# Mix weights of the first two blocks from one on-chip table, quantizer units in their order of use, block 1's gate and up products beside block 0's

## The chip, the core and the metric

The kernel runs on one core of one Trainium2 chip. TensorE multiplies, VectorE (DVE) and ScalarE (ACT) do the work on rows, GpSimd (POOL) has small jobs, SyncE (SP) and ScalarE issue the transfers. The metric is the time of one execution in microseconds on the device. Lower is better.

## The reference, cut to what matters

```python
x: (64 samples, 64 channels, 512)           # 4096 rows of 512
# layer 0
y  = einsum('bct,bcd->bdt', x, weights[subjects])      # each sample has one of 8 64x64 matrices
w  = ternary_quant(w_gate_up), ternary_quant(w_proj)   # groups of 64: mean of |w|, sign, scale
h  = silu(gate) * up                                   # hidden size 2048
x  = x + rms_norm(h) @ wq_p.T
# layer 1
H  = x @ W.T + adapter (rank 16, one of 8 per sample)
x  = x + sum over 8 experts of c[t, e, o] * (H @ expert_w[e].T + expert_b[e])
     # c: softmax of a 4096-column router, top 2 of 8, renormalized
```

## The kernel before, in words

The rows are worked in 8 blocks of 512 (`NBLK`). Stage A, some 850 us, computes layer 0 for a block and, behind it, the layer-1 linear of the block before. The router and the experts follow and are not touched. All float products are made of high and low halves ("hi" and "lo"), which ScalarE (hi) and VectorE (lo) split off.

A block is: `mix` (the sample matrices, two uses of a PSUM slot), then for each of the 16 hidden chunks j `gu(i, j)` (16 matmuls, gate and up), `silu` of the gate on ScalarE, the product on VectorE, the split of the product (`high`, `low`), its square and the running sum (`square`, `squares`), and `proj(i, j)` (8 matmuls) into four PSUM banks. At the end come `squares(i)` (TensorE's sums over columns), the variance, `power` on GpSimd, the residual, `turn` (transposes), `adapt` and two `linear` halves for layer 1.

**Blocks 0 and 1 are special.** The weights arrive unquantized. `UNITS` lists 24 units of 1,024 columns: "up" j (the gate and up weights of chunk j) and "down" (projection weights of two chunks). A unit is loaded, ScalarE makes magnitude and sign (`quant_in`), TensorE the group mean (`quant`, 2 matmuls), VectorE the scale (`quant_scale`, or `quant_floor` where ScalarE has copied the mean out in `quant_mean`), two gap instructions (`quant_gap`) and three more (`quant_sign`), and ScalarE writes the result out (`quant_out`). The loop over `h` in `range(PAIRS)` (8 passes) does this for three units a pass, with the `gu` and `proj` of block 0 for two chunks. Block 1's `gu` rides along one pass late: pass h has `gu(0, 2h)`, `gu(1, 2h - 2)`, `gu(0, 2h + 1)`, `gu(1, 2h - 1)`; the last two (`AHEAD = 2`) come after the loop. Block 1's products are kept as tiles `hid1` in a ring of 6; ten of them go to memory (`keep_hid`) and are fetched again (`fetch_hid`). After the loop TensorE projects block 1 in the order `SECOND_ORDER` (chunks 10 to 14, then 0 to 9, then 15): `proj(1, p)`. Positions 5 to 14 take fetched tiles.

**What sets the order.** Every engine's program is written out by hand; an engine works strictly in that order. `slot` is a ring of two PSUM slots; `FIRST`, `SECOND`, `REST` number its uses. A use n waits until `drained` counts n - 1, that is, until the use two before it is read out (`take`). For instance the `gu` of chunk 1 uses the slot of the fourth group mean.

**Mix weights.** `mixw` (block 0) and `mixw1` (block 1) are block-diagonal, one 64x64 matrix for each sample. `gather_mix` on SyncE reads a sample's index into a register (`value_load`) and issues one 16 KB transfer from memory (L452, L454); four of block 0's eight come from GpSimd in the same way (L691, L693).

**Transfers.** SyncE has the units' loads, the gathers, `keep_hid` and, at the end of the loop, this sequence (L500 to L509), which the change leaves alone:

```python
for r in range(5):
    fetch_hid(r)
sp.wait_ge(w_lo_ready, 3)          # wc_lo of linear_weights is written
sp.dma_start(x_mix[:, :, :], one(XB, 2)).then_inc(xmix_in, 16)
gather_mix(2, mixw, mixw_in)
for r in range(5, HC - RING):
    fetch_hid(r)                   # tile of position 5 + r
```

`linear_weights` splits the layer-1 weights, which lie in `x_mix`, into `wc_hi` and `wc_lo`; `small_weights` does the adapter's.

## Time and profile before

| | us |
|---|---|
| median of 3 runs | 2211.55 (2211.19 to 2212.24) |
| the profiled execution | 2213.71 |
| its span | 2212.0 |
| TensorE busy | 2193.9 (99%) |
| VectorE busy | 1625.1 (73%) |
| ScalarE busy | 1053.5 (48%) |
| GpSimd busy | 63.8 (3%) |

TensorE is busy nearly throughout, so the time is its instructions plus what it loses at the start and in a few waits. Two stretches differ from the rest: the first 40 us, in which the first weights have to arrive, and the quantizing loop (to about 177 us), in which VectorE is nearly full too. "Granted clock" is the share of 2.4 GHz that TensorE got: 1.00 or 0.50.

### The profile page before, as it was taken

Reading aid. Unit: us, or ns where it says so; the run is one execution under the profiler, and the core shown is the slowest. Engines: PE = TensorE matmul, PEld = TensorE weight load, DVE = VectorE, ACT = ScalarE, POOL = GpSimd, SP = SyncE. Lnnn points to the kernel's source line nnn. Section 1 sums busy time; section 2 is a strip of 40 time slices with the busy share of each in tenths; the row PEclk is TensorE's granted clock in tenths of the full one; section 3 lists DMA queues with packets and bytes.
Section 4 is the critical chain, followed back from the end, with each engine's and each line's share of the span. In section 5 each row is a group of like instructions: output and inputs, shape, how many; then the busy total and the mean of one; then the engine's idle time right before and its main releaser. Section 6 shows DMA issues by size and latency. Waiting matters only on the chain.

```text
span 2212.0 us, 28768 instructions
## 1 busy us (share of the span) xinstructions
PE 2193.9 (99%) x9817; PEld 1810.9 (82%) x9817; DVE 1625.1 (73%) x2119; ACT 1053.5 (48%) x1493; POOL 63.8 (3%) x83
## 2 busy tenths in 40 slices
PE   7999999999999999999999999999999999999999
PEld 5778888888888888888888888888888888888887
DVE  8986444444444445689999999999898888888883
ACT  6764333333333233588777878777332222222221
POOL 0000000101111102000000000000000000000000
PEclk9999999999999999999999999999999999999999
DMA  6313303232424224412212121116222222222220
GB/s 210 105 53 126 98 20 105 83 107 81 111 80 109 92 58 143 157 67 81 81 71 85 71 85 71 63 68 262 103 100 85 81 85 81 95 71 100 66 85 24
DMA packets 157908, 205.66 MB, mean 93 GB/s; under 512 B 63330, under 2 KB 96674, under 8 KB 155682
## 3 DMA queue, kind: packets, MB, share of 16 engines
q1 hardware_dynamic: 114578, 149.95, 20.5%
q10 hardware_dynamic: 43152, 55.06, 7.6%
q8 instruction: 22, 0.36, 0.1%
q14 instruction: 28, 0.23, 0.0%
q0 software_dynamic: 128, 0.07, 0.0%
HBM read 136.35 MB, written 68.68 MB: 93 GB/s over the span
## 4 chain that ended last, share of the span: by engine, by line
PE 94%; issue 4%; DVE 1%; POOL 1%; ACT 0%; DMA 0%; POOLq 0%; DVEq 0%; ACTq 0%
PE slot L1657 19%; PE ex_bank L1834 10%; PE ex_bank L1833 10%; PE ex_bank L1832 10%; PE pj L1670 9%; PE high_bank L1799 5%; PE high_bank L1803 5%; PE high_bank L1801 5%; PE low_bank L1799 4%; PE low_bank L1803 4%; PE low_bank L1801 4%; PE slot L1719 3%; PE slot L1626 1%; PE slot L1708 1%; PE ex_bank L1847 1%
## 5 line engine op out<-in xcount | busy, mean ns | idle before, releaser
L1657 PE MATMUL slot<-y_hi,wgu 128*128 128x512 f32 x1024 | 402.5, 393 | 1.2 <-ACT wgu L768 0.6
L1657 PE MATMUL slot<-y_lo,wgu 128*128 128x512 f32 x1024 | 399.3, 390 | 0.0
L1832 PE MATMUL ex_bank<-ew_hi,hb 128*128 128x512 f32 x992 | 385.9, 389 | 0.0
L1833 PE MATMUL ex_bank<-ew_hi,hb 128*128 128x512 f32 x992 | 385.9, 389 | 0.0
L1834 PE MATMUL ex_bank<-ew_lo,hb 128*128 128x512 f32 x992 | 385.9, 389 | 0.0
L1104 ACT ACTIVATE ex_bank<-eb_sb 128x512 f32<-128x512 f32 x248 | 149.3, 602 | 451.1 <-DVE acc L1563 391.5
L1513 DVE SCALAR_TENSOR_TENSOR lead_in<-code_in,wts 128x1024 bf16<-128x1024 bf16 x256 | 311.7, 1218 | 7.5 <-ACT wts L1044 5.8
L1657 PEld LDWEIGHTS slot<-y_hi,wgu 128*128 128x128 f32 x1024 | 192.8, 188 | 44.8 <-DVE q_scale L1174 2.9
L1657 PEld LDWEIGHTS slot<-y_lo,wgu 128*128 128x128 f32 x1024 | 192.7, 188 | 39.8
L1216 DVE TENSOR_TENSOR hid<-gate,slot 128x512 f32<-128x512 f32 x112 | 76.9, 687 | 192.0 <-ACT gate L784 191.3
L1832 PEld LDWEIGHTS ex_bank<-ew_hi,hb 128*128 128x128 f32 x992 | 186.2, 188 | 38.7
L1833 PEld LDWEIGHTS ex_bank<-ew_hi,hb 128*128 128x128 f32 x992 | 186.2, 188 | 38.6
L1834 PEld LDWEIGHTS ex_bank<-ew_lo,hb 128*128 128x128 f32 x992 | 186.2, 188 | 38.6
L784 ACT ACTIVATE gate<-slot 128x512 f32<-128x512 f32 x128 | 76.3, 596 | 276.5 <-PE slot L1657 237.3
L1799 PE MATMUL high_bank<-rw_hi,hb 128*128 128x512 f32 x512 | 199.3, 389 | 0.0
L1803 PE MATMUL high_bank<-rw_lo,hb 128*128 128x512 f32 x512 | 199.2, 389 | 0.0
L1801 PE MATMUL high_bank<-rw_hi,hb 128*128 128x512 f32 x512 | 199.2, 389 | 0.0
L1563 DVE SCALAR_TENSOR_TENSOR acc<-ex_bank,c_ring,acc 128x512 f32<-128x512 f32 x193 | 144.6, 749 | 66.0 <-PE ex_bank L1834 63.2
L1670 PE MATMUL pj<-wpj,hid_hi 128*128 128x512 f32 x484 | 190.1, 393 | 0.0
L1670 PE MATMUL pj<-wpj,hid_lo 128*128 128x512 f32 x484 | 188.4, 389 | 0.0
L1799 PE MATMUL low_bank<-rw_hi,hb 128*128 128x512 f32 x384 | 149.4, 389 | 0.0
L1801 PE MATMUL low_bank<-rw_hi,hb 128*128 128x512 f32 x384 | 149.4, 389 | 0.0
(169 smaller groups left out, 3500.8 us busy)
## 6 DMA issues: line engine op xcount, KB each, us to landing
hb<-h_scratch SPq DMA_DIRECT2D x34, 512.0 KB, 3.3
code_scratch<-half_code SPq DMA_DIRECT2D x32, 512.0 KB, 2.6
half_in<-code_scratch SPq DMA_DIRECT2D x32, 512.0 KB, 3.3
hb<-h_scratch ACTq DMA_DIRECT2D x30, 512.0 KB, 3.6
h_scratch<-ht ACTq DMA_DIRECT2D x48, 256.0 KB, 3.0
q_raw<-in_w_ffn SPq DMA_DIRECT2D x21, 512.0 KB, 3.4
x_scratch<-x_res ACTq DMA_DIRECT2D x8, 1024.0 KB, 4.5
lead_scratch<-lead SPq DMA_DIRECT2D x32, 256.0 KB, 2.0
```

The lines of the kernel that those rows point to most:

```text
L1104: nc.scalar.activation(ex[e][:, :], eb_sb[:, e, :], ACT.Copy).then_inc(ex_seeded, 1)
L1216: nc.vector.tensor_tensor(hid[:, j % 2, :], gate[:, g, :], slot[s % 2][:, 1, :], ALU.mult).then_inc(drained, 1)
L1513: nc.vector.scalar_tensor_tensor(lead_in[:, k % 2, :].bitcast(BF16).rearrange("p (a n) -> p a n", a=2), code_in[:, k % 2, :, :], float(2 * ...
L1563: nc.vector.scalar_tensor_tensor((res if e == E - 1 and not first else acc)[:, u, :], ex[e][:, :], c_ring[:, k, e:e + 1], (xin if e == 0 e ...
L1657: last = mm(slot[s % 2][:, g, :], wgu[:, c, r * P:(r + 1) * P], y[:, c, :], start=(c == 0 and v == 0), stop=(c == DC - 1 and v == 1))
L1670: last = mm(pj[k][:, :], h[:, k * P:(k + 1) * P], wpj[:, w, :], start=(j == 0 and v == 0), stop=(j == HC - 1 and v == 1))
L1799: mm(plane[k][:, :], hb[:, u, c, 0, :], rw_hi[:, k, c, :], start=False, stop=False, skip_group_check=True)
L1801: mm(plane[k][:, :], hb[:, u, c, 1, :], rw_hi[:, k, c, :], start=False, stop=False, skip_group_check=True)
L1803: last = mm(plane[k][:, :], hb[:, u, c, 0, :], rw_lo[:, k, c, :], start=False, stop=True, skip_group_check=True)
L1832: mm(ex[e][:, :], hb[:, u, c, 0, :], ew_hi[:, e, c, :], start=False, stop=False, skip_group_check=True)
L1833: mm(ex[e][:, :], hb[:, u, c, 1, :], ew_hi[:, e, c, :], start=False, stop=False, skip_group_check=True)
L1834: last = mm(ex[e][:, :], hb[:, u, c, 0, :], ew_lo[:, e, c, :], start=False, stop=(c == DC - 1), skip_group_check=True)
```

## The change

- **Table.** The whole table of 8 matrices is loaded once into each half of the partitions (two transfers of 128 KB, pieces of 256 bytes). For blocks 0 and 1 the matrices are then copied on chip with a register as index: four samples on VectorE, twelve on GpSimd. The twelve transfers of SyncE and the four of GpSimd go. Blocks 2 to 7 gather as before.
- **Loads.** SyncE issues block 1's rows (`x_res`) as soon as unit 0 has landed, and unit 2 behind them; ScalarE's queue keeps units 0 and 1 and `x_mix`.
- **Units** stand in the order up 2h, up 2h + 1, down h.
- **Order.** Both mixes come before unit 1's group mean. `gu(1, j)` follows `gu(0, j)` at once, in every pass, and `AHEAD` is gone. ScalarE copies two group means a pass. In the first pass VectorE puts block 1's low halves between gap and sign of unit 1, and all of unit 2 behind the first two products.
- **PSUM.** The first blocks use `slot_first` and `pj_first` (block 1's mix is written into the latter, with the semaphores `mix1_filled` and `mix1_drained`); later uses have them in exchanged places. `bank` chooses. The router's and experts' banks are renamed to match.
- **Second block.** Without `gu` behind the loop, `proj(1, 0)` follows the sums of squares. The residual of block 0 is put between the low halves; `small_weights` goes into the loop, `linear_weights` from before position 4 to behind position 6; `turn`, `adapt` and `linear` on TensorE move from positions 1, 2, 5, 7, 10 to 3, 4, 8, 10, 13.

```diff
-UNITS = [u for j in range(HC) for u in ([("up", j), ("down", j // 2)] if j % 2 == 0 else [("up", j)])]
+UNITS = [u for h in range(HC // 2) for u in (("up", 2 * h), ("up", 2 * h + 1), ("down", h))]
...
-FIRST = ["q0", "q1", "mix0@0", "mix1@0", "q2"]
+FIRST = ["q0", "mix0@0", "mix1@0", "q1"]
...
+    FIRST += [f"gu{_j}@0", f"gu{_j}@1"]
+    FIRST += ["q2"] if _h == 0 else []
     FIRST += [f"q{k}" for k in quant_of(_h)[:2]]
...
+    FIRST += [f"gu{_j + 1}@0", f"gu{_j + 1}@1"]
     FIRST += [f"q{k}" for k in quant_of(_h)[2:]]
```

SyncE's program:

```diff
-            sp.wait_ge(dconst, 2)
-            sp.wait_ge(subject_in, 16)
-            gather_mix(0, mixw, mixw_in, range(SPB // 2))
+            for r in range(0, P, C):
+                sp.dma_start(table[r:r + C, :, :], cond_w.rearrange("(v r) k -> r v k", r=C)).then_inc(table_done, 16)
...
+            sp.wait_ge(qraw_in[0], 16)
             sp.dma_start(x_res[:, :, :], one(XB, 1)).then_inc(xmix1_in, 16)
-            gather_mix(1, mixw1, mixw1_in, range(3))
+            sp.dma_start(q_raw[:, 2, :], w_ffn[2]).then_inc(qraw_in[2], 16)
```

GpSimd's (VectorE has the same for its four samples, before unit 0):

```diff
+            pool.wait_ge(table_done, 32)
+
+            def choose(i, w, samples, done):
+                for q in samples:
+                    v = pool.value_load(subject_i[0:1, i * SPB + q:i * SPB + q + 1], min_val=0, max_val=E - 1)
+                    r = (q % 2) * C
+                    nc.gpsimd.tensor_copy(w[r:r + C, q // 2, r:r + C],
+                                          table[r:r + C, bass.ds(v, 1), :].rearrange("p z k -> p (z k)")).then_inc(done, 1)
+
+            choose(0, mixw, range(SPB // 2, SPB), first_chosen)
+            choose(1, mixw1, range(SPB), second_chosen)
```

TensorE's:

```diff
             quant(0)
             again(9)
+            mix(0)
+            second_mix()
             quant(1)
-            mix(0)
-            quant(2)
...
                 gu(0, j)
-                if h:
-                    gu(1, j - 2)
+                gu(1, j)
+                if h == 0:
+                    quant(2)
...
                 gu(0, j + 1)
-                if h:
-                    gu(1, j - 1)
-                else:
-                    mix(1)
+                gu(1, j + 1)
                 proj(0, j)
...
-            for j in range(HC - AHEAD, HC):
-                gu(1, j)
             for p in range(HC - 1):
                 proj(1, p, SECOND_ORDER[p])
-                if p in (1, 2):
-                    turn(0, p - 1)
-                if p == 5:
+                if p in (3, 4):
+                    turn(0, p - 3)
+                if p == 8:
                     adapt(0)
-                if p == 7:
+                if p == 10:
                     linear(0, 0)
-                if p == 10:
+                if p == 13:
                     linear(0, 1)
```

The order of ScalarE and VectorE is shown as their instructions stand. In the names, `y_hi` and `y_lo` are halves of a mix, `gate` is a silu, `q_mag` and `q_sign` a `quant_in`, `wgu` and `wpj` a `quant_out`.

ScalarE at the start, before, from unit 0's write-out to block 0's first gate and the two write-outs behind it:

```order
L768 ACTIVATE wgu<-q_res 128x4x256
L747 ACTIVATE y_hi<-slot 128x1024 x2
L754 ACTIVATE q_mag<-q_raw 128x1024
L755 ACTIVATE q_sign<-q_raw 128x1024
L754 ACTIVATE q_mag<-q_raw 128x1024
L755 ACTIVATE q_sign<-q_raw 128x1024
L754 ACTIVATE q_mag<-q_raw 128x1024
L755 ACTIVATE q_sign<-q_raw 128x1024
L784 ACTIVATE gate<-slot 128x512
L771 ACTIVATE wpj<-q_res 128x1024
L768 ACTIVATE wgu<-q_res 128x4x256
```

The same place in the change:

```order
L755 ACTIVATE y_hi<-slot_first 128x1024 x2
L783 ACTIVATE wgu<-q_res 128x4x256
L762 ACTIVATE y_hi<-pj_first 128x1024 x2
L769 ACTIVATE q_mag<-q_raw 128x1024
L770 ACTIVATE q_sign<-q_raw 128x1024
L783 ACTIVATE wgu<-q_res 128x4x256
L769 ACTIVATE q_mag<-q_raw 128x1024
L770 ACTIVATE q_sign<-q_raw 128x1024
L769 ACTIVATE q_mag<-q_raw 128x1024
L770 ACTIVATE q_sign<-q_raw 128x1024
L799 ACTIVATE gate<-slot_first 128x512
L818 ACTIVATE sq<-hid 128x512
```

The first gate had no write-out before it but unit 0's; now unit 1's `wgu` and the `quant_in` of units 3 and 4 behind it stand ahead of it.

VectorE at the start, before, from block 0's low halves of the mix to the second scale behind the first product:

```order
L1167 TENSOR_TENSOR y_lo<-slot,y_hi 128x1024 x2
L1174 TENSOR_SCALAR q_scale<-slot 128x1024
L1187 TENSOR_TENSOR q_gap<-q_scale,q_mag 128x1024
L1191 TENSOR_TENSOR q_res<-q_gap,q_mag 128x1024
L1197 TENSOR_TENSOR q_gap<-q_gap,q_mag 128x1024
L1199 TENSOR_TENSOR q_res<-q_res,q_gap 128x1024
L1202 TENSOR_TENSOR q_res<-q_res,q_sign 128x1024
L1216 TENSOR_TENSOR hid<-gate,slot 128x512
L1174 TENSOR_SCALAR q_scale<-slot 128x1024
```

The same place in the change:

```order
L1200 TENSOR_TENSOR y_lo<-slot_first,y_hi 128x1024 x2
L1214 TENSOR_SCALAR q_scale<-slot_first 128x1024
L1227 TENSOR_TENSOR q_gap<-q_scale,q_mag 128x1024
L1231 TENSOR_TENSOR q_res<-q_gap,q_mag 128x1024
L1207 TENSOR_TENSOR y_lo<-pj_first,y_hi 128x1024 x2
L1237 TENSOR_TENSOR q_gap<-q_gap,q_mag 128x1024
L1239 TENSOR_TENSOR q_res<-q_res,q_gap 128x1024
L1242 TENSOR_TENSOR q_res<-q_res,q_sign 128x1024
L1256 TENSOR_TENSOR hid<-gate,slot_first 128x512
L1264 TENSOR_TENSOR hid<-gate,slot_first 128x512
L1214 TENSOR_SCALAR q_scale<-slot_first 128x1024
L1227 TENSOR_TENSOR q_gap<-q_scale,q_mag 128x1024
```

Unit 1 is now done around block 1's low halves, and unit 2 (here its first two instructions) moved behind both first products.

VectorE in the second block, before, from the sum of position 3 to the low half of position 4 (`hid1` is block 1's tile; L1160 is `wc_lo`):

```order
L1249 TENSOR_TENSOR sumsq<-sumsq,sq 128x512
L1224 TENSOR_TENSOR hid1<-gate,slot0 128x512
L1143 TENSOR_TENSOR a_lo<-a_raw,a_hi 128x512
L1145 TENSOR_TENSOR b_lo<-b_raw,b_hi 128x512
L1149 TENSOR_SCALAR adapter_i<-adapter_i 128x1
L1150 CAST lmask<-idx_i 128x64
L1152 CAST adapter_f<-adapter_i 128x1
L1154 TENSOR_SCALAR lmask<-lmask,adapter_f,scal_sb 128x64
L1160 TENSOR_TENSOR wc_lo<-x_mix,wc_hi 128x2048
L1238 TENSOR_TENSOR hid_lo<-hid1,hid_hi 128x512
```

And in the change, from the low half of position 4 (L1194 is `wc_lo`):

```order
L1278 TENSOR_TENSOR y_lo<-hid1,y_hi 128x512
L1289 TENSOR_TENSOR sumsq<-sumsq,sq 128x512
L1278 TENSOR_TENSOR y_lo<-hid1,y_hi 128x512
L1289 TENSOR_TENSOR sumsq<-sumsq,sq 128x512 x3
L1278 TENSOR_TENSOR hid_lo<-hid1,hid_hi 128x512
L1289 TENSOR_TENSOR sumsq<-sumsq,sq 128x512
L1194 TENSOR_TENSOR wc_lo<-x_mix,wc_hi 128x2048
L1278 TENSOR_TENSOR hid_lo<-hid1,hid_hi 128x512
```

The split of the layer-1 weights stood before position 4's low half and now stands behind position 6's sum.

## Rows read from the trace of the kernel before

**Rows 1.** TensorE's waits, whole run: us in total, times, longest.

```profile
PE slot L1708 <- DVE x1t_lo L1279: 1.1, 1, 1.1
...
PE pj L1670 <- DVE y_lo L1238: 0.7, 1, 0.7
```

**Rows 2.** Windows: busy us of PE, PEld, DVE, ACT, POOL; clock; DMA.

```profile
68.40:88.00 19.60, 19.60 (x88) 15.30 (x86) 17.77 (x27) 14.12 (x18) 0.00 (x0) 1.00 0.32 107
...
20.00:21.00 1.00, 0.93 (x3) 0.59 (x4) 0.24 (x1) 1.00 (x2) 0.00 (x0) 0.50 0.08 16
```

**Rows 3.** Chain that ended last, to 120 us: start, us, what.

```profile
7.19 5.04 DMA mixw<-in_cond_w
...
38.92 7.54 PE slot L1657 x32
...
56.61 1.81 PE pj L1670 x8
...
58.87 7.27 PE slot L1657 x32
```

**Rows 4.** TensorE in order of time: start, us, instruction [idle before].

```profile
6.23 3.83 PE L1643 MATMUL slot<-q_mag,group_mean 128*128 128x512 bf16 x9
...
20.52 0.99 PE L1657 MATMUL slot<-y_hi,wgu 128*128 128x512 f32 x1
...
32.26 3.73 PE L1626 MATMUL slot<-mixw,x_res 128*128 128x128 f32 x32
```

**Rows 5.** DMA issues of 13.5 to 20 us: count, KB each, us to landing.

```profile
mixw<-in_cond_w SPq DMA_DIRECT2D x5, 16.0 KB, 2.0
```

**Rows 6.** SyncE's issues in order of time, first 50 us.

```profile
3.14 4.36 SPq L454 DMA_DIRECT2D mixw<-in_cond_w  x4
```

**Rows 7.** ScalarE in order of time, first 50 us.

```profile
25.90 0.60 ACT L784 ACTIVATE gate<-slot 128x512 f32<-128x512 f32 x1 [1.24 <-PE slot L1657]
...
30.09 1.05 ACT L754 ACTIVATE q_mag<-q_raw 128x1024 bf16<-128x1024 f32 x1
31.04 1.05 ACT L755 ACTIVATE q_sign<-q_raw 128x1024 bf16<-128x1024 f32 x1
```

**Rows 8.** VectorE in order of time, first 50 us.

```profile
6.47 1.22 DVE L1174 TENSOR_SCALAR q_scale<-slot 128x1024 bf16<-128x1024 f32 x1 [3.96 <-PE slot L1636]
...
36.51 2.36 DVE L1167 TENSOR_TENSOR y_lo<-slot,y_hi 128x1024 fp32r<-128x1024 f32 x2
...
40.83 1.22 DVE L1174 TENSOR_SCALAR q_scale<-slot 128x1024 bf16<-128x1024 f32 x1
...
43.60 0.69 DVE L1197 TENSOR_TENSOR q_gap<-q_gap,q_mag 128x1024 bf16<-128x1024 bf16 x1
...
45.06 0.69 DVE L1202 TENSOR_TENSOR q_res<-q_res,q_sign 128x1024 bf16<-128x1024 bf16 x1
```

**Rows 9.** The chain that ended last, 140 to 270 us.

```profile
177.93 7.42 PE slot L1657 x32
...
199.16 3.00 PE slot L1708 x12
```

**Rows 10.** SyncE's issues in order of time, 182 to 208 us.

```profile
193.67 0.43 SPq L506 DMA_DIRECT2D x_mix<-in_x  x1
```

**Rows 11.** ScalarE in order of time, 150 to 265 us.

```profile
184.85 0.64 ACT L803 ACTIVATE sq<-hid 128x512 f32<-128x512 f32 x1 [0.65 <-DVE sumsq L1249]
...
186.25 0.64 ACT L803 ACTIVATE sq<-hid 128x512 f32<-128x512 f32 x1 [0.24 <-DVE sumsq L1249]
...
188.30 1.90 ACT L740 ACTIVATE wc_hi<-x_mix 128x2048 fp32r<-128x2048 f32 x1
...
207.35 0.63 ACT L795 ACTIVATE y_hi<-hid 128x512 fp32r<-128x512 f32 x1 [2.75 <-DMA hid<-hid_scratch]
```

**Rows 12.** VectorE in order of time, 150 to 265 us.

```profile
179.35 2.73 DVE L1273 SCALAR_TENSOR_TENSOR x_res<-pj,inv,x_res 128x512 f32<-128x512 f32 x4 [1.22 <-POOL inv L707]
...
190.35 2.28 DVE L1160 TENSOR_TENSOR wc_lo<-x_mix,wc_hi 128x2048 fp32r<-128x2048 f32 x1
```

More of the change, by code:

```diff
@@ L69 @@
 RING = 6
-AHEAD = 2
-GU_ORDER = []
-FIRST = ["q0", "q1", "mix0@0", "mix1@0", "q2"]
+GU_ORDER = [(i, j) for j in range(HC) for i in range(2)]
+FIRST = ["q0", "mix0@0", "mix1@0", "q1"]
 PAIRS = HC // 2
```

317 lines of the change are left out of this document (184 added, 133 removed).

## The prediction

> **What bounds the kernel now.** I read the waits of TensorE first: from 40 us to the middle of the run it has two waits worth a line, 1.1 us for the split `x1t_lo` and 0.7 us for a low half [rows 1]. A period of the quantizing loop takes 19.6 us, and TensorE is busy for all of it, VectorE for 17.77 us of it [rows 2]. So past 40 us TensorE is the bound: a microsecond it loses there is lost at the end. Ahead of that the chain that ended last shows what can be won. The last gather of mix weights is issued at 7.19 and lands 5.04 us later, at 12.2, and the third pair of `gu` products starts at 38.92 us, after which nothing is late [rows 3]. Behind the first stage, from 177.93 us on, the second block is projected.
>
> So I measure the change at two points: when TensorE is through with the first pass of the loop, and how long it takes from the sums of squares (177.93) to block 2.
>
> **First point, what is equal work.** In the new order the first pass has both blocks' `gu` of both indices, where the old one has block 0's alone; the mix of block 1 is in both. So it carries two more `gu`, 7.27 us by the row of a pair [rows 3]. The old pass is through at 38.92; the new one breaks even at 38.92 + 7.27 = 46.2.
>
> **When the new chain can start.** TensorE's nine filling matmuls end at 10.06, and a mix at full clock takes 3.73 us [rows 4]. Both mixes and the second group mean now stand in front of everything: 10.06 + 2 × 3.73 + 0.45 = 18.0 us is the earliest for the mean of unit 1; call this moment Q. Later it is if the weights are. The table is two transfers, issued behind the index row by about 1.7 us. A 16 KB gather took 2.0 us on quiet queues and 5.04 us amid the large loads [rows 3, 5], so the table, 16 times as large in all and amid the same loads, lands at 3.7 at the earliest and at about 6.0 as I take it, with 8 as the upper end. GpSimd then does twelve samples. No row shows a load of a register followed by a copy; SyncE does four samples of load and DMA in 4.36 us, 1.09 each [rows 6], which I take as the upper end, and a bit over half of it as the lower (0.6, without the DMA itself). I take 0.78, as the copy is small: 6.0 + 12 × 0.78 = 15.4. Then the second mix at a clock between the two levels, 4.6 us, and the mean: Q = 20.5. Bounds 18.0 and 26 (8 + 12 × 1.09 + 4.6 + 0.5).
>
> A rule bears on the 6.0. The row shows a 16 KB gather at 5.04 us behind large loads [rows 3]. The Trainium skill, "DMA: Bandwidth & Descriptors", section "Queues, rings and completion order", has every DMA engine take turns between the queues packet by packet, by which a small transfer on SyncE's queue would hardly wait for ScalarE's loads. By it the table would land near 3.7 and the time be 2 us less than I forecast.
>
> **What is queued behind Q.** VectorE: scale and two gaps of unit 1, 2.77 us; then both low halves of block 1 and the signs of unit 1, from 36.51 to 40.83 in the old trace, 4.32 us [rows 8]. That is Q + 7.1. ScalarE, in its new order, waits for this with `quant_out(1)`, and behind it stand two `quant_in`: five instructions of 0.95 each [rows 7], then the first gate, 0.60: Q + 12.5. In the old order nothing stood between `gu` and the gate (25.90, straight at the end of `gu`) [rows 7]. Then the product 0.7, the square 0.5 on ScalarE, the second gate 0.6 and its product 0.6 to 0.7: Q + 15.0. Now VectorE starts all of unit 2: 2.77 us and then from 43.60 to 45.75, 4.92 in all [rows 8]: Q + 19.9. ScalarE writes unit 2 out (0.95) and copies the mean of unit 3, VectorE floors it (1.5 for both, as I estimate from ScalarE's 1.05 for the same 1,024 columns): Q + 22.4. Only then is the slot free for `gu(0,1)`, since a use waits until the use two before it is drained. TensorE has by then done two `gu` and three means, under 9 us of work, so it waits, most of it in one piece of 5 to 6 us before this `gu`. From here two pairs' worth of work in a row: 7.27 + 2.26 (projection and mean [rows 3]) = 9.5. After a wait the granted clock was 0.50, the 1.2 GHz level, from 20 to 21 us [rows 2], and the `gu` begun at 20.52 was done at 25.90, 5.4 against 3.6 us [rows 4, 7]: +1.7. The pass ends at Q + 33.7, with Q = 20.5 at **54.2, 8.0 us behind**. The best of all bounds, Q = 18.0 and a warm clock, gives 50.0: still 3.8 behind. The worst, Q = 26, gives 59.7: 13.5 behind.
>
> What this chain hides: the four copies that VectorE now does before unit 0 end near 9.4, so unit 0 starts there instead of at 6.47 [rows 8] and is done at 14.3, but it is not needed before Q. The gathers taken off SyncE, the moved loads and the index row cost nothing for the same reason. In the later passes ScalarE copies one more mean out of PSUM (1.05) and spares VectorE a scale of 1.22 [rows 8] for a shorter one; both keep slack in the 19.6 us, and TensorE stays the bound, so nothing is given back. The new homes of the PSUM tiles move no work.
>
> **Second point, from the sums of squares on.** Call 177.93 S. The old order has two `gu` there, 7.42 us [rows 9]; now they are done before. To the end of the adapter product (202.16) TensorE took 24.23; without the 7.42 and the 1.1 wait it is 15.7 [rows 1, 9] for six projections, two turns and the product. The new order has the projections 6 to 9 as well before projection 10, 4 × 1.81 = 7.25 [rows 3]: TensorE could start projection 10 at S + 22.95. In the old order the first half of the linear layer stands ahead of projection 10 as well, which the new one has behind it.
>
> What projection 10 needs is a hidden tile that comes back from memory. SyncE fetches the first five, then waits for `wc_lo`, loads `x_mix` (193.67), gathers eight samples and fetches the rest only then [rows 10]; ScalarE's high half of tile 10 stood until 207.35, idle before it for 2.75 us for just this transfer [rows 11]. From the load of `x_mix` to it: 13.68 us. SyncE's program is not changed there. But when is `wc_lo` ready? Residuals to S + 4.1 [rows 12], first sum of squares 0.4, then squares and sums take turns between ScalarE and VectorE at 1.40 us a tile (184.85 to 186.25 [rows 11]) up to tile 6: S + 12.1. Then `wc_hi` 1.90 and `wc_lo` 2.28 [rows 11, 12], moved from before tile 4 to behind tile 6: S + 16.4 (old: 192.63, S + 14.7). Then 13.68, a high half 0.63 and a low half 0.7: projection 10 starts at S + 31.5, 8.55 us after TensorE was ready. A smaller wait for tile 7 behind `wc_lo` (about 2 us) is inside it. With a wait of over 5 us comes the low clock again, +1.7. Against it stand the two waits removed, 1.85 [rows 1]. Sum: 8.55 + 1.7 − 1.85 = **8.4 us behind**. Bounds: 4 (the squares take turns faster and clock stays up) and 10.
>
> Together 16.4 us. The profiled execution took 2213.7 us (span 2212.0) and becomes 2230.1; the median of the three runs lies 2.2 us lower, so 2228.0.
>
> **Rivals.** (a) The other side, faster: the chain behind Q does not form, because the gates find ScalarE free as in the old trace. The gain is then the start of the first mix, 12.48 to 10.06, 2.4 us, one low-clock start of 1.7, the two waits of 1.85: 2206. Its point of decision is Q below 46.2 − 32.0 = 14.2, and two mixes do not fit before that; nothing in the rows speaks for it. (b) Only the first pass is late: the tiles come back in time, if `wc_lo` came by S + 7.8. Then the two waits are won: 8.0 − 1.85, 2218. Against it: 1.40 a tile. (c) Only the second point is late, the pass being hidden by VectorE's slack: 2220. Against it: after 40 us TensorE has no slack. (d) It does not do what it says, as TensorE has the same instructions in both: 2211.5.
>
> **How the numbers follow.** Forecast 0.80, (a) 0.05, (b) 0.07, (c) 0.05, (d) 0.03. The likeliest gives 2228, its own bounds 2219 (3.8 + 4) to 2235 (13.5 + 10). The range takes in (b): 2218 to 2235. A measurement of this kernel tells 0.2%, 4.4 us, from no change. Faster by more: 0.05; within: 0.03; slower: 0.92.
>
> **What would show it.** Right: the first gate about 12 us after the mean of unit 1, a wait of TensorE of 5 to 6 us before `gu(0,1)`, the third pair of `gu` near 54 us; in the second block a wait of several us before projection 10 whose chain goes over the transfer from `hid_scratch`, and the granted clock at 0.50 behind both. Wrong: a first gate at the end of its `gu`, a third pair before 46 us, or hidden tile 10 present when projection 9 ends.

## The result, and the profile after

The changed kernel takes 2236.9 us (median of four runs, 2236.1 to 2238.5), the kernel before, run beside it, 2211.4: a ratio of 1.0117 with a 95% interval of 1.0102 to 1.0131. It is 25.5 us slower. The sign and the two places were forecast; the forecast was 2228.0, 16.4 us above the 2211.55 of before, and the upper end of the range 2235, so the time lies outside it.

The profiled execution of the changed kernel took 2236.07 us with a span of 2233.9, 21.9 above the 2212.0 of before. TensorE's waits up to block 2 (columns: us in total, times, longest); behind the first 40 us the old kernel had two worth a line [rows 1]:

```profile
PE pj L1745 <- DVE hid_lo L1278: 8.4, 2, 6.0
PE slot_first L1701 <- ACT q_mag L769: 5.2, 1, 5.2
PE slot_first L1724 <- DVE q_scale L1220: 5.1, 1, 5.1
PE slot_first L1680 <- DVE mixw L1172: 4.6, 1, 4.6
PE slot_first L1701 <- DVE hid L1256: 4.1, 1, 4.1
PE slot_first L1724 <- DVE y_lo L1207: 1.5, 1, 1.5
PE slot_first L1701 <- DVE hid L1264: 0.8, 1, 0.8
PE slot_first L1724 <- DVE q_scale L1214: 0.6, 1, 0.6
...
```

The first pass, in the chain that ended last (start, us, what); it answers to [rows 3]:

```profile
1.95 8.31 DMA table<-in_cond_w
...
14.01 6.15 PE slot_first L1680 x32
20.15 3.57 PE pj_first L1690 x32
23.78 0.39 PE slot_first L1701
24.20 1.24 DVE q_scale L1214
...
32.19 1.04 ACT q_mag L769
...
36.07 0.49 ACT gate L799
...
44.97 1.02 ACT q_scale L777
46.01 0.44 DVE q_scale L1220
...
46.49 8.99 PE slot_first L1724 x32
...
57.75 6.36 PE slot_first L1724 x28
```

The table is there at 10.3 us, four copies of VectorE later the first mix starts at 14.0, and the mean of unit 1 is taken up at 24.2: that is Q. The first mix takes 6.15 us and the second 3.57, for the same 32 matmuls. TensorE had stood for 4.6 us before the first, and until 18 us its granted clock was 0.50, the 1.2 GHz level; GpSimd's last copy, for the second mix, ended at 19.4, before the first mix was done (busy us of PE, PEld, DVE, ACT, POOL; granted clock; DMA; then start, us, instruction):

```profile
14.00:15.00 1.00, 0.99 (x5) 1.00 (x5) 1.00 (x1) 0.00 (x0) 0.47 (x2) 0.50 1.00 397
```

```profile
19.16 0.24 POOL L698 COPY mixw<-table 64x64 f32 x1 [0.32 <-issue]
```

The first gate stands behind two units read in, at Q + 11.9. The wait of 5.1 us ends with unit 3's scale, `gu(0,1)` starts at Q + 22.3, and its two `gu` take 8.99 us instead of 7.27. The third pair starts at 57.75, 11.55 behind the 46.2 at which the new order breaks even.

The second block, from the same chain; it answers to [rows 9 to 12]:

```profile
196.41 0.80 PE slot_first L1754 x8
...
209.52 1.91 ACT wc_hi L749
211.45 2.30 DVE wc_lo L1194
213.77 0.38 SPq L508
...
225.14 2.82 DMA hid<-hid_scratch
...
229.39 3.78 PE pj L1745 x8
233.17 3.17 PE slot L1794 x12
...
261.07 4.11 PE slot L1724 x17
```

The sums of squares end at S = 197.2. At 213.77 SyncE comes through its wait for `wc_lo`, issues block 2's load and eight gathers, and only then the fetch of the tile that projection 10 needs. That projection starts at 229.39, at half clock, by the windows:

```profile
229.00:230.00 1.00, 0.61 (x2) 0.52 (x3) 1.00 (x3) 0.68 (x3) 0.00 (x0) 0.50 0.96 352
230.00:233.00 3.00, 3.00 (x9) 2.32 (x8) 2.21 (x4) 1.64 (x3) 0.00 (x0) 0.50 0.21 80
```

In the order of the old kernel, with its two late `gu` counted in, S is 177.93 + 7.42 = 185.35, and from there to block 2's first `gu` (239.3) it is 54.0 us. In the new one S is 197.2 and the rest 63.9. So 11.9 us are lost up to S and 9.9 behind it, 21.8 of the 21.9 of the span; from block 2's first `gu` to the end it is 1972.6 to 1972.9 us in every trace of this document.

### The profile page after: what moved, and what is told of

Its sections match the earlier page's. It is cut to its first block, busy times and chain, and to the rows that moved or that the text cites. A ratio compares the mean times of both kernels' runs of the same rounds, so it can differ in the third digit from the quotient of the medians.

```text
span 2233.9 us, 28759 instructions
## 1 busy us (share of the span) xinstructions
PE 2197.8 (98%) x9809; PEld 1813.0 (81%) x9817; DVE 1621.6 (73%) x2123; ACT 1063.3 (48%) x1500; POOL 68.2 (3%) x91
## 4 chain that ended last, share of the span: by engine, by line
PE 91%; issue 4%; DVE 2%; ACT 1%; POOL 1%; DMA 0%; SPq 0%; ACTq 0%; DVEq 0%; POOLq 0%
PE slot L1724 13%; PE ex_bank L1905 10%; PE ex_bank L1904 10%; PE ex_bank L1903 10%; PE pj L1745 7%; PE low_bank L1870 5%; PE low_bank L1874 5%; PE low_bank L1872 5%; PE slot_first L1724 5%; PE high_bank L1870 4%; PE high_bank L1874 4%; PE high_bank L1872 4%; PE slot L1794 3%; PE pj_first L1745 1%; PE slot L1680 1%
## 5 line engine op out<-in xcount | busy, mean ns | idle before, releaser
L1724 PE MATMUL slot<-y_hi,wgu 128*128 128x512 f32 x768 | 299.4, 390 | 0.2 <-DVE y_lo L1200 0.2
L1724 PE MATMUL slot<-y_lo,wgu 128*128 128x512 f32 x768 | 298.9, 389 | 0.0
L1870 PE MATMUL low_bank<-rw_hi,hb 128*128 128x512 f32 x512 | 199.3, 389 | 0.0
L1874 PE MATMUL low_bank<-rw_lo,hb 128*128 128x512 f32 x512 | 199.2, 389 | 0.0
L1872 PE MATMUL low_bank<-rw_hi,hb 128*128 128x512 f32 x512 | 199.2, 389 | 0.0
L1745 PE MATMUL pj<-wpj,hid_hi 128*128 128x512 f32 x416 | 163.7, 394 | 8.4 <-DVE hid_lo L1278 8.4
L799 ACT ACTIVATE gate<-slot 128x512 f32<-128x512 f32 x96 | 57.3, 597 | 237.5 <-PE slot L1724 198.4
L1724 PEld LDWEIGHTS slot<-y_hi,wgu 128*128 128x128 f32 x768 | 144.2, 188 | 30.1 <-DVE y_lo L1200 0.2
L1724 PEld LDWEIGHTS slot<-y_lo,wgu 128*128 128x128 f32 x768 | 144.2, 188 | 29.8
L1745 PE MATMUL pj<-wpj,hid_lo 128*128 128x512 f32 x416 | 162.9, 391 | 0.0
L1870 PE MATMUL high_bank<-rw_hi,hb 128*128 128x512 f32 x384 | 149.4, 389 | 0.0
L1872 PE MATMUL high_bank<-rw_hi,hb 128*128 128x512 f32 x384 | 149.4, 389 | 0.0
```

The costliest lines, as they stand in the source:

```text
L1724: last = mm(bank(n, s)[:, g, :], wgu[:, c, r * P:(r + 1) * P], y[:, c, :], start=(c == 0 and v == 0), stop=(c == DC - 1 and v == 1))
L1745: last = mm(sums[:, k, :], h[:, k * P:(k + 1) * P], wpj[:, w, :], start=(j == 0 and v == 0), stop=(j == HC - 1 and v == 1))
L1870: mm(plane[k][:, :], hb[:, u, c, 0, :], rw_hi[:, k, c, :], start=False, stop=False, skip_group_check=True)
L1872: mm(plane[k][:, :], hb[:, u, c, 1, :], rw_hi[:, k, c, :], start=False, stop=False, skip_group_check=True)
L1874: last = mm(plane[k][:, :], hb[:, u, c, 0, :], rw_lo[:, k, c, :], start=False, stop=True, skip_group_check=True)
```

## The experiments

Spans are those of the profiled executions, times the medians; the kernel before, run beside them in every group, had 2211.5 to 2211.7. Because the start of a run shifts by up to 1 us between executions (the table's landing is 10.3 in one, 10.8 in another), I compare by three points: Q, the third pair of `gu` counted from Q, and the stretch from S to block 2's first `gu`.

| kernel | time us | span | Q | third pair | S | S to block 2 |
|---|---|---|---|---|---|---|
| before, two `gu` added | 2211.4 | 2212.0 | | 46.2 | 185.4 | 54.0 |
| changed | 2236.9 | 2233.9 | 24.2 | Q + 33.6 | 197.2 | 63.9 |
| hidden tiles fetched first | 2228.5 | 2226.5 | 24.9 | Q + 33.8 | 198.2 | 55.4 |
| same, and late split | 2226.0 | 2223.9 | 25.2 | Q + 33.8 | 198.5 | 52.6 |
| same as two above, low half on GpSimd | 2231.1 | 2229.1 | 24.5 | Q + 33.5 | 197.5 | 58.7 |
| gates first | 2230.5 | 2228.8 | 23.8 | Q + 28.1 | 191.4 | 64.6 |
| fillers | 2235.4 | 2232.8 | 25.2 | Q + 32.1 | 196.7 | 63.3 |
| table with unit 0 alone in flight | 2235.1 | 2232.3 | 22.4 | Q + 33.6 | 195.4 | 64.0 |
| table first on the queue | 2232.5 | 2230.7 | 20.2 | Q + 34.0 | 194.0 | 64.0 |
| gathers, no table | 2230.9 | 2229.7 | 19.3 | Q + 34.3 | 193.0 | 63.9 |
| all edits, split on GpSimd | 2218.2 | 2216.7 | 19.3 | Q + 24.6 | 184.1 | 59.7 |
| all edits, late split | 2213.1 | 2210.9 | 19.4 | Q + 25.9 | 185.6 | 52.6 |
| same, and four stores on SyncE | 2212.5 | 2210.1 | 19.3 | Q + 25.8 | 185.3 | 52.2 |

**The fetch behind the gathers.** SyncE's lines, moved:

```diff
-            for r in range(5):
+            for r in range(HC - RING):
                 fetch_hid(r)
             sp.wait_ge(w_lo_ready, 3)
             sp.dma_start(x_mix[:, :, :], one(XB, 2)).then_inc(xmix_in, 16)
             gather_mix(2, mixw, mixw_in)
-            for r in range(5, HC - RING):
-                fetch_hid(r)
```

> One line of the second step undone: SyncE fetches all ten hidden tiles from memory before it waits for `wc_lo` and loads for block 2, so that nothing stands between the squares and the tile that projection 10 needs. In the changed kernel TensorE waits 5.99 us before projection 10, and the low clock behind it costs 2.0 us in that projection and 0.45 us in the linear layer. My theory (the place of the fetch behind SyncE's wait and eight gathers is the whole wait) expects both gone: 8.4 us less than the changed kernel, a span of 2225.5 us; the wait of 2.4 us before projection 7 stays. The rival (the squares that take turns between ScalarE and VectorE at 1.40 us a tile and the split of the linear weights are late anyway) expects the wait to turn up again at a square or a high half: 3 us less at most, a span above 2230.5.

From S to block 2 it took 55.4 us for 63.9, 8.4 less, as expected; the span fell by 7.4 because this execution's S came 1.0 later, 0.7 of it at Q. Of TensorE's waits on low halves of the second block, the one of 6 us is gone:

```profile
PE pj L1743 <- DVE hid_lo L1276: 2.4, 1, 2.4
PE pj L1743 <- DVE y_lo L1276: 0.2, 1, 0.2
```

Both slow products behind it are gone as well, and the squares did not take its place. The first explanation holds: most of the second loss is the order of lines in SyncE's program that the change leaves alone.

**The split of the linear weights.** Two ways, both on top of the fetch. First the low half on GpSimd:

```diff
-                nc.vector.tensor_tensor(wc_lo[:, :, :], x_mix[:, :, :], wc_hi[:, :, :].bitcast(F32), ALU.subtract)...
...
+            nc.gpsimd.tensor_tensor(wc_lo[:, :, :], x_mix[:, :, :], wc_hi[:, :, :].bitcast(F32), ALU.subtract)...
```

> The order of fetches on SyncE as in the run where all tiles are fetched first (2228.5 us, span 2226.5), and the low half of the linear weights, 2.29 us on VectorE behind tile 6, made on idle GpSimd. TensorE's wait of 2.4 us before projection 7 is what the two splits of the linear weights put into the squares. If VectorE's part of it is what is late, 2.0 to 2.4 us go (span about 2224.3); if ScalarE's 1.91 us of `wc_hi` alone keeps the square of tile 7 as late, 0.5 us at most (span above 2226); if GpSimd takes over 12 us for it or slows VectorE on their way to memory, the linear layer waits and the run is longer.

It is 3.3 us longer from S to block 2 than the fetch alone. GpSimd's and VectorE's rows in order of time (start, us, instruction, idle before it):

```profile
211.78 4.51 POOL L725 TENSOR_TENSOR wc_lo<-x_mix,wc_hi 128x2048 fp32r<-128x2048 f32 x1 [12.59 <-ACT wc_hi L749]
```

```profile
209.15 0.69 DVE L1277 TENSOR_TENSOR hid_lo<-hid,hid_hi 128x512 fp32r<-128x512 f32 x1
...
212.25 4.59 DVE L1277 TENSOR_TENSOR hid_lo<-hid,hid_hi 128x512 fp32r<-128x512 f32 x1 [1.63 <-ACT hid_hi L810]
```

The same instruction of VectorE takes 0.69 us at 209.15 and 4.59 at 212.25; it begins inside GpSimd's subtraction (211.78 to 216.29) and ends 0.55 behind it. TensorE waits 4.6 us for it. Of the three expectations the last came true in its second half: GpSimd slowed VectorE. It took 4.5 us itself, not over 12, and what waited was projection 7 and not the linear layer. The Trainium skill, "SBUF — State Buffer", section "SBUF: two separate sides", says that GpSimd and a VectorE operation with two SBUF inputs exclude each other for the whole instruction; this row agrees.

Then both splits behind tile 9 on their old engines:

```diff
-                if p == 6:
-                    linear_weights()
                 if p in (7, 8):
                     turn(0, p - 7)
+                if p == 9:
+                    linear_weights()
```

> All hidden tiles fetched first, as in the run with span 2226.5, and both splits of the linear weights behind tile 9 instead of tile 6, on the same engines. The squares' 1.40 us a tile stand against TensorE's 1.81 a projection and 2.72 for the adapter behind projection 8, so slack grows from tile to tile; behind tile 9 it should hold the 2 us of the splits, and TensorE's wait of 2.4 us before projection 7 goes: span 2224.0. If a wait of 1 us or more shows up before projection 10 instead, the slack was less; if nothing is gained, the splits were not what made projection 7 wait. On GpSimd the same subtraction took 4.5 us, and a low half of VectorE beside it 4.60 us for 0.70, which is why it is back on VectorE here.

Span 2223.9 for 2224.0 expected. From S to block 2 it takes 52.6 us, 2.8 less than with the fetch alone. Four projections, those between the second turn and the adapter product, where the wait of 2.4 us stood, are now one piece of the chain, at 1.89 us each:

```profile
209.70 7.57 PE pj L1743 x32
```

52.6 is 1.4 us less than the 54.0 of the kernel before, whose order takes 53.9 in the run with the table in the old order below: the second part of the new order is good, with these two places mended.

**ScalarE's order in the first pass.**

```diff
             quant_in(2)
-            quant_out(1)
+            silu(0, 0)
             quant_in(3)
+            silu(1, 0)
+            quant_out(1)
             for h in range(PAIRS):
...
-                silu(0, j)
+                if h:
+                    silu(0, j)
...
-                silu(1, j)
-                if h == 0:
-                    quant_out(2)
+                if h:
+                    silu(1, j)
                 if more:
                     quant_mean(3 * h + 3)
+                if h == 0:
+                    quant_out(2)
```

> ScalarE's order in the first pass alone: the two first gates stand ahead of the writing out of unit 1 and the reading in of unit 4, and the copy of unit 3's mean ahead of the writing out of unit 2. Nothing is added or left out. My theory (the chain unit 1, writing out, reading in, gate, product, unit 2 on ScalarE and VectorE sets the pass) expects the first product 6 us earlier, TensorE's wait of 5.1 us before `gu(0,1)` gone or under 1 us... with `gu(0,1)` at about 14 to 15 us behind the mean of unit 1 instead of 22.3, and the third pair of `gu` at about 26 behind it instead of 33.6: 7 to 8 us less than the changed kernel, span 2226 to 2227. The rival (VectorE's own work, two units, two low halves and two products, sets it, whatever ScalarE's order) expects 2 us at most, span above 2231.

The third pair comes at Q + 28.1 for 33.6, 5.5 us earlier; expected were 7 to 8. The chain shows the rest: `gu(0,1)` starts at 39.41, Q + 15.6 (14 to 15 expected), but its two `gu` now take 10.23 us:

```profile
39.41 10.23 PE slot_first L1729 x32
```

That is 3.0 us over 7.27. Before that pair TensorE was busy for 1.38 of the 3 us from 33 and for 0.09 of the 3 us from 36, by the windows, and from 39 to 45 the granted clock was 0.50, the 1.2 GHz level. ScalarE's order was the cause of 6.7 us (Q + 22.3 less Q + 15.6), and 1.2 of them went to the clock.

**The price of the clock.** Eighteen idle matmuls in the changed kernel's wait:

```diff
                 if more:
                     quant(3 * h + 4)
+                if h == 0:
+                    for r in range(18):
+                        mm(pj_first[:, r % SUB, :], wgu[:, 0, 0:P], y_hi[:, 0, :], start=True, stop=True)
```

> Eighteen matmuls of no use, of 0.23 us each at full clock, in TensorE's wait of 5.1 us before `gu(0,1)`, into PSUM that is free there; the rest is the changed kernel. It measures the disputed price of the low clock behind that wait. If the clock is what makes the next two `gu` 8.99 us instead of 7.27, they take 7.3 us and the kernel is 1.7 us shorter (span 2232.2). If the clock falls all the same, the fillers run at the low level and end behind the wait: no gain, or up to 2 us lost (span 2234 to 2236).

```profile
42.33 5.17 PE pj_first L1826 x18
47.50 7.51 PE slot_first L1724 x32
```

The fillers took over the start at the low level (the windows have the granted clock at 0.50 from 40 to 43 and at 1.00 from 45), and the pair starts at Q + 22.3 as before and takes 7.51 us for 8.99; the third pair is 1.4 us earlier from Q. The span fell by 1.1 us, as its Q came 1 us later and its wait before projection 10 was 1 us shorter (5.0). The clock is the cause of most of the 1.7.

**Why the table landed at 10.3.** Three runs. In the first the other loads wait:

```diff
             act.dma_start(q_raw[:, 0, :], w_ffn[0]).then_inc(qraw_in[0], 16)
+            act.wait_ge(table_done, 32)
             act.dma_start(x_mix[:, :, :], one(XB, 0)).then_inc(xmix_in, 16)
...
             sp.wait_ge(qraw_in[0], 16)
+            sp.wait_ge(table_done, 32)
             sp.dma_start(x_res[:, :, :], one(XB, 1)).then_inc(xmix1_in, 16)
```

> ScalarE and SyncE hold their large loads (both blocks' input, units 1 and 2) until the table of mix weights has landed; only unit 0 is under way beside it. In the changed kernel the table took 8.31 us and landed at 10.26 us, where I had put 6.0. Theory one, the table waits behind the large loads: it lands at 4 to 5 us, GpSimd's twelve copies of 0.68 us are done by about 13.5, the mean of unit 1 is there at 18 to 19 instead of 24.2, and the kernel is 5 us shorter (span about 2229). Theory two, the table's 512 pieces of 256 bytes take that long by themselves: it still lands near 9 to 10, the inputs land 3 us or more behind it, and the kernel is as long or up to 3 us longer (span 2234 to 2237).

The table's median time from issue to landing, of the changed kernel and then of this one:

```profile
table<-in_cond_w SPq DMA_DIRECT2D x2, 128.0 KB, 8.3
```

```profile
table<-in_cond_w SPq DMA_DIRECT2D x2, 128.0 KB, 3.8
```

So the pieces of 256 bytes are not what takes 8.3 us; ScalarE's and SyncE's large loads beside them are. But Q gained only 1.8 us, and not by the table. Block 0's input, issued at 5.62 instead of about 1.2 us, now held the first mix:

```profile
5.62 8.89 DMA x_mix<-in_x
...
14.55 3.84 PE slot_first L1682 x32
```

The mix starts 0.5 us later than in the changed kernel and ends 1.8 earlier, as it takes 3.84 us for 6.15: the fillers ran until 14.0, so TensorE stood for only 0.5 us before it. Unit 1, for which ScalarE waited 6.5 us (to 16.57), was read in by 18.6 and did not hold Q, since its mean stands behind both mixes (to 21.96). The expectation of the next run, written before I read this chain so, puts the lost gain down to unit 1.

In the second nothing is held, and the table only stands first on ScalarE's queue:

```diff
-            for r in range(0, P, C):
-                sp.dma_start(table[r:r + C, :, :], ...).then_inc(table_done, 16)
...
+            for r in range(0, P, C):
+                act.dma_start(table[r:r + C, :, :], ...).then_inc(table_done, 16)
             act.dma_start(q_raw[:, 0, :], w_ffn[0]).then_inc(qraw_in[0], 16)
```

> The table's two transfers stand first on ScalarE's queue, ahead of unit 0, block 0's input and unit 1, instead of on SyncE's queue beside them; no engine waits for more than before. With the other large loads held back the table took 3.8 us, where it took 8.3 beside them, but that run lost the gain again since unit 1 then came 5 us later. Theory (a transfer at the head of the queue is served first, and the rest is behind it by little): the table lands by 5.0, the twelve copies of GpSimd are done by 13.5, the first mix starts at 10 to 11.5 and the mean of unit 1 is there at 19 to 20 instead of 24.2; the kernel is 4 to 5 us shorter, span 2229 to 2230. Rival (the loads together are limited by bandwidth, so what the table gains the input of block 0 or unit 1 loses): the first mix waits for its input till 12 or later, the gain is under 2 us, span above 2232.

```profile
table<-in_cond_w ACTq DMA_DIRECT2D x2, 128.0 KB, 3.1
```

```profile
2.18 4.50 DMA q_raw<-in_w_ffn
...
12.60 3.57 PE slot_first L1680 x32
...
20.21 1.24 DVE q_scale L1214
...
42.50 9.41 PE slot_first L1724 x32
...
54.17 7.27 PE slot_first L1724 x32
```

Q is 20.2 for 24.2. The first mix starts 1.4 us earlier; it is held by the nine fillers and not by the table, as unit 0 is issued 1.4 us later and the fillers behind its mean end at 12.6. The other 2.6 us are the first mix itself, 3.57 us for 6.15 with no wait before it. The span is 3.2 us shorter (4 to 5 expected): the pair behind the wait of 5.1 us took 9.41 us for 8.99, and 0.35 more went on the way to S. Since ScalarE's large loads are issued 1.4 us later here, the run does not tell the place in the queue from the head start. It comes near the forecast's own case: the third pair starts at 54.17, where I had put 54.2. That is in part luck, as Q is 0.3 us before the 20.5 that I had put, by another path, and the rest 0.3 longer.

In the third there is no table at all. The sixteen samples of the two blocks are gathered from memory, four of each block by SyncE and four by GpSimd; the rest is the new order:

```diff
-            for r in range(0, P, C):
-                sp.dma_start(table[r:r + C, :, :], ...).then_inc(table_done, 16)
+            sp.wait_ge(dconst, 2)
+            sp.wait_ge(subject_in, 16)
+            gather_mix(0, mixw, gathered, range(SPB // 2))
...
             sp.wait_ge(qraw_in[0], 16)
             sp.dma_start(x_res[:, :, :], one(XB, 1)).then_inc(xmix1_in, 16)
+            gather_mix(1, mixw1, gathered1, range(SPB // 2))
```

> One part of the change undone: no table; the sixteen samples are gathered from memory as in the kernel before, four of each block by SyncE and four of each by GpSimd, in the new order of everything else. By the rows of the kernel before SyncE issues four in 4.4 us and each takes about 5 to land, so block 1's last is issued at about 12.5 and is there at 17 to 18. If the on-chip copying pays in the new order, the mean of unit 1 comes later than the 24.2 us it has with the table (26 or later: the gathers of both queues stuck behind the loads, span 2235 or more). If it costs, since the table itself landed at 10.3, the mean comes at 21 to 22 and the kernel is 2 to 3 us shorter (span 2231 to 2232).

```profile
12.71 2.22 DMA mixw<-in_cond_w
15.02 3.81 PE pj_first L1678 x32
...
19.30 1.24 DVE q_scale L1200
```

Q is 19.3, 4.9 us before that of the table, and the span 4.2 us shorter. Both gains are larger than I had put for this side: the last gather took 2.2 us and not 5, at a time when the large loads were nearly through (the core's transfers moved 43 GB/s from 12.7 to 14.3 us), and the first mix, at a granted clock of 1.00, took 3.81 us for 6.15.

**The table in the old order.**

```diff
-            gather_mix(0, mixw, mixw_in, range(SPB // 2))
+            for r in range(0, P, C):
+                sp.dma_start(table[r:r + C, :, :], ...).then_inc(table_done, 16)
```

with the four copies on VectorE and twelve on GpSimd, as in the changed kernel, and no gather for block 1. SyncE also waits for unit 0 before it loads block 1's rows, as in the changed kernel.

> The kernel before with one part of the change: the mix weights of the first two blocks copied on chip out of the table (SyncE's load, four copies on VectorE, twelve on GpSimd, as in the changed kernel), all orders as before. If the table costs only the later start of the first mix (14.0 for 12.5 us), the kernel is 1.5 us longer (span 2213.5). If VectorE's four copies that wait for the table are the cost, because units 0 and 1 are quantized behind them and both stand ahead of the low half of the mix in this order (from 13.9 us on instead of 6.5), the first `gu` starts at 24 to 25 instead of 20.5 and the kernel is 3 to 5 us longer (span 2215 to 2217). That the table is worth something here (SyncE free for the loads) would show as a span below 2212.

```profile
1.94 9.79 DMA table<-in_cond_w
...
15.37 1.24 DVE q_scale L1191
...
27.94 5.26 PE slot L1675 x16
...
46.21 7.55 PE slot L1675 x32
```

2221.2 us, span 2219.3: 7.3 us over the kernel before, and the third pair is late by the same 7.3 (46.21 for 38.92). I had expected 3 to 5. The second theory holds and was too mild: the table landed at 11.7 in this order, VectorE began unit 0 at 15.37 instead of 6.47 [rows 8], and the first `gu` came at 27.9 instead of 20.5 [rows 4].

**Everything together.** All edits on the changed kernel: fetch first, table first, gates first, unit 3's scale ahead of unit 2's signs, fillers in TensorE's three waits there, six fillers instead of nine at the start, and the low half on GpSimd. What is new on VectorE, ScalarE and TensorE:

```diff
                 if h == 0:
-                    quant(2)
-                if more:
+                    quant_scale(2)
+                    quant_gap(2)
+                    quant_floor(a)
+                    quant_sign(2)
+                elif more:
                     quant_floor(a)
...
+                if h == 0:
+                    quant_mean(3)
                 act.wait_ge(drained, use(0, f"gu{j}")[0] + 1)
                 square(0, j, hid[:, j % 2, :])
...
+                    idle(3)
                     quant(3 * h + 3)
...
+                    idle(2)
                     quant(3 * h + 4)
...
+                    idle(13)
-            again(9)
+            again(6)
```

> Everything together that the runs point to, on the changed kernel: all hidden tiles fetched first (8.4), the table first on ScalarE's queue and three fewer filling matmuls at the start (4 to 5), the gates first in ScalarE's order (5.5 in its run), fillers of 0.23 us in TensorE's waits there to keep the clock (2.8: the two `gu` behind took 10.23 us for 7.4), unit 3's scale ahead of unit 2's signs (1.5), and the low half of the linear weights on GpSimd (0 to 2.4). If the terms are independent, 22 to 26 us go of the changed kernel's span of 2233.9: 2208 to 2212, level with the kernel before (2212.0) or up to 4 us below it. If they share a path (table and gates above all, both ahead of `gu(0,1)`), 3 to 5 us of it are missing and it stays above 2213.

2218.2 us, ratio 1.0030 (1.0019 to 1.0041). The terms of the first pass add up nearly in full: S is at 184.1, 13.1 us earlier, for 13.8 to 14.8 expected, and 1.3 ahead of the old kernel's 185.4 (that of one execution 2.2 us above its median, as the next section says). What is missing is behind S, where the form on GpSimd costs its 4.6 us of wait and a slow pair of projections. The next version undoes that, has the splits behind tile 9, and tries more: three fillers at the start, unit 2's mean, scale and gaps ahead of the second `gu` and its product, and on ScalarE unit 4 read in ahead of the second gate. The fillers in the three waits, 3, 2 and 13 in the version above, are 0, 5 and 1 in it.

```diff
-    FIRST += [f"gu{_j}@0", f"gu{_j}@1"]
+    FIRST += [f"gu{_j}@0"]
     FIRST += ["q2"] if _h == 0 else []
+    FIRST += [f"gu{_j}@1"]
...
-            again(6)
+            again(3)
...
-            silu(1, 0)
             quant_out(1)
+            quant_in(4)
+            silu(1, 0)
```

> The version with everything in it once more (span 2216.7), with four edits: the splits of the linear weights on VectorE and ScalarE behind tile 9 (2.6 for the slow GpSimd form and 2.4 for the wait), three fewer filling matmuls at the start, as block 0's input has landed by then (1.1), unit 2's mean and scale ahead of the second `gu` and its product, and unit 4 read in ahead of the second gate (2.3: `gu(0,1)` about 11.5 us behind the mean of unit 1 instead of 13.9). If these hold, 8.4 us go: span 2208.3, 3.7 us or 0.17% below the kernel before. If VectorE is by now the bound of the first pass (its chain runs unbroken from 33 to 54 us in that run), the last 2.3 and perhaps the 1.1 come to nothing: span 2210.5 to 2212, level with it.

2213.1 us, ratio 1.0008 (0.9999 to 1.0017): level with the kernel before, not under it. Behind S it takes 52.6 us, 7.1 less than with GpSimd's form, for 5.0 expected. The new edits of the first pass cost instead of gaining: S is 1.5 later. Unit 2's mean ahead of the second `gu` moves that `gu` one use back in the ring of slots, so it has to wait until block 0's first product is made, which I had overlooked:

```profile
27.09 0.80 PE L1736 MATMUL slot_first<-y_hi,wgu 128*128 128x512 f32 x1 [3.59 <-DVE hid L1263]
```

It starts 3.6 us late and runs slow after the wait (5.45 us for 3.9). And with three fillers the first mix started at 10.04 instead of 11.34, but took 5.36 us instead of 3.57, though the granted clock is 1.00 in its windows. From 11 to 13 us it did 7 matmuls a us, where that of the version above did 10 to 12 and that of the changed kernel, at 0.50, 6 to 7. Why, no run here tells.

Last, four stores of block 0's rows on SyncE instead of ScalarE:

```diff
-            store_h(0, 1)
+            copy_h(0, 1)
...
+            sp.wait_ge(drained, n + 1)
+            for b in range(2):
+                for v in range(2):
+                    sp.dma_start(HB[0, 2 + b, v], ht[:, b, v, :]...).then_inc(h_stored, 16)
```

> As the run of all edits with the late splits, and four stores of block 0's second half of rows issued by SyncE instead of ScalarE, where they stood 2.4 us in front of the high half of block 2's mix; TensorE waits behind that mix for 2.4 us in every kernel so far, the kernel before too. If these issues are that wait, 2 us go; if the mix's low half and its slot are late anyway, under 0.5 us.

2212.5 us, ratio 1.0007 (0.9998 to 1.0016). The stretch behind S is 0.4 us shorter (52.2 for 52.6), within the under 0.5 of the second expectation. The premise of 2.4 us was wrong: in the trace of the kernel before TensorE does not wait at all between block 2's mix and its first `gu`, and in the version without the moved stores it waits 0.17 us there. No version here is faster than the kernel before.

## Why the prediction was wrong in size, point by point

**What bounds the kernel, and what is equal work: right.** A microsecond lost in the first pass is lost at the end. The break-even of 46.2 and that of S, 185.35, carry the whole account: 11.9 + 9.9 = 21.8 of the 21.9 us of span.

**When the new chain can start: this step failed.** I put the table's landing at 6.0, nearest to the 16 KB gather at 5.04 us amid the loads [rows 3], with 8 as the upper end; it was 10.3, outside. A gather of 16 KB is no measure for the table's two transfers of 128 KB beside the large loads: one took 8.3 us there, 3.8 with only unit 0 in flight, and 3.1 when both were issued ahead of the large loads on their queue.

The path behind the landing was another one, too. I had GpSimd's twelve copies hold the second mix. They came every 0.68 to 0.71 us (0.78 forecast) and were done at 19.4, before the first mix was. What held Q was VectorE's four copies, 0.77 us apart, and behind them a first mix at half clock, for which my sum has no term (I had put the clock into the second mix, at 0.9 us): 10.26 + 3.75 + 6.15 + 3.57 + 0.45 = 24.2, for 20.5. From the landing to Q this is 13.9 us where my sum has 14.5. That the two are so near is luck, as my sum follows a path that nothing waited for. So of the 3.7 us of Q the landing is 4.3 and the rest gives 0.6 back. The third pair came 3.6 late (57.75 for 54.2).

What I made of the rule of turns would have moved the forecast the wrong way: the table at 3.7 instead of 6.0, and it was 10.3. The Trainium skill's "DMA: Bandwidth & Descriptors", section "Queues, rings and completion order", has each engine take turns between the queues packet by packet. No run here shows the turns; but that by them a transfer on SyncE's queue hardly waits for large loads is not so here: it took 8.3 us beside ScalarE's three loads and, from 4.0 us on, SyncE's own, and 3.8 beside one of them.

**What is queued behind Q: right.** The first gate came at Q + 11.9 (forecast 12.5), the wait before `gu(0,1)` was 5.1 us (5 to 6), that `gu` started at Q + 22.3 (22.4), the clock cost 1.7 (1.7), the third pair Q + 33.6 (33.7). The run with the gates first shows that ScalarE's order is the cause of 6.7 of the 22.3 us up to `gu(0,1)`, and the fillers that the clock is that of 1.5 of the 1.7.

**"In the later passes nothing is given back": right but for 0.3.** Up to S the loss grew from 11.55 to 11.9 us. The small weights, now converted inside the loop ahead of its last unit, make TensorE wait 0.6 us for that unit's scale. I had not followed `small_weights()` to its new place.

**Second point: right, a little short.** Projection 10 started at S + 32.2 (31.5), the waits ahead of it are 8.6 us (6.0, 2.4 and 0.2; 8.55 forecast), the two of the old kernel are gone as forecast, TensorE's work ahead of projection 10 is 0.6 us longer than I had it, and the clock cost 2.4 us (1.7), as both the projection (3.78 for 1.81) and the linear layer behind it (3.17 for 2.72) ran slow. 9.9 for 8.4. The run with all tiles fetched first takes 8.4 of it away.

**From the profiled execution to the median: the second step that failed.** I took the 2.2 us by which the profiled execution of before lay above its median off the forecast as well. But that gap was one execution's own: its span was 2212.0 with a mean clock of 0.998, where 21 executions of the same kernel beside the last experiments lie between 2208.5 and 2210.3 with 0.999 to 1.000. The profiled execution of the changed kernel lay 0.8 below its own median. So 3.2 us of the 25.5 are in neither trace: 22.4 us separate the profiled times, 25.5 the medians. Where the 2.2 us of the old kernel's execution lay can be narrowed down. From S to block 2 its order takes 53.9 us in the run with the table in the old order as well, and behind that all traces agree within 0.3 us. So they lay ahead of S, and an execution of the usual span of 2209.8 should reach S at about 183.1 instead of 185.35; this is an estimate (2209.8 - 1972.7 - 54.0), no such execution was traced. Against it even the version with all edits, at 184.1, is behind.

Of the 8.9 us that were missing, 3.6 are the start of the chain, 0.3 the loop, 1.5 the stretch behind S, 3.2 the step from profile to median, and 0.2 to 0.3 roundings. The rivals (b), (c) and (d) fall, since both points cost time (11.9 and 9.9 us). So does (a), with Q at 24.2 where it needed 14.2. But that figure holds only for ScalarE's order as it was: with all edits the third pair starts at 43.9, 2.3 ahead of the break-even point, with a Q of 19.3.

What stays open: at a granted clock of 1.00 the first mix took 3.57 us in the two kernels with six or nine fillers just before it, and 5.36 and 4.91 in the two with three. And I have not undone the order of units, the PSUM places or the mixes' place ahead of unit 1's mean by themselves; what each of them costs or gives is not shown.

## What to carry to other kernels

Price a transfer by its size and by what is in flight beside it, and take the nearest row as a lower end, not as the middle, when that row moves an eighth as much. A small transfer that everything waits for should be under way before the large ones: issued first on their queue it took 3.1 us here, on a queue of its own beside them 8.3. When one engine waits for two paths, add up both. A late start can cost twice, here 4.6 us of wait and 2.6 in a mix at half clock behind it. When an order is changed on one engine, walk through every other engine's order for what now stands in front of the first use: here an order that the change left alone (SyncE's fetches) cost 8.4 us and one that it made (ScalarE's gates) 5.5. And before a trace serves as the measure, compare its time with the other executions of the same kernel.

## What I had not expected of the hardware

- A subtraction of 128x2048 on GpSimd (4.51 us) held up a VectorE instruction that began 0.47 us later: 4.59 us instead of 0.69. Work given to an idle GpSimd was not free while VectorE had a subtraction of two tiles to do.
- A transfer of 128 KB in pieces of 256 bytes took 3.1 us when issued ahead of the large loads, 3.8 with one load of 512 KB beside it, and 8.3 to 9.9 beside the large loads of two queues.
- The price of a low clock behind a wait was not a constant. Behind the wait of 5.1 us before `gu(0,1)` it was 1.7 us in the changed kernel and up to 2.5 in the others that have this wait (9.72 us for the pair with the gathers), 2.6 behind the 4.6 us before the first mix, 2.4 behind the 6.0 before projection 10, and 3.0 behind one of 3.3 us, in the run with the gates first. Fillers took back 1.5 of the 1.7.
